# Keys in memory as three parts, maxima ahead of the operand loads, and a prologue that loads step 0 first

## The reference

```python
# x: 16 x 256 x 128, ctx: 16 x 1601 x 128; 16 heads of depth 8; all f32
qh, kh, vh = heads(layernorm(x) @ wq.T + bq), heads(ctx @ wk.T + bk), heads(ctx @ wv.T + bv)
attn = softmax(qh @ kh.T / sqrt(8))                 # per batch and head: 256 x 1601
x = x + tanh(g_xattn) * ((attn @ vh) @ wd.T + bd)
n = layernorm(x)
scores = sigmoid(n @ gate_W) * route_scale          # 8 experts, the best 2 of them
gate = one_hot_weights(top_k(scores, 2))            # divided by their sum
x = x + tanh(g_ffn) * (sum_e gate_e * (gelu(n @ W1_e + b1_e) @ W2_e + b2_e) + gelu(n @ Ws1 + bs1) @ Ws2 + bs2)
```

## Time and profile before

| | |
|---|---|
| median of three runs | 1434.74 us |
| profiled execution, own time | 1436.73 us |
| its span | 1434.9 us |
| PE busy | 1241.7 us (87%) |
| DVE busy | 1049.3 us (73%) |
| ACT busy | 1055.6 us (74%) |
| POOL busy | 418.7 us (29%) |
| mean granted clock of TensorE | 0.902 |
| moved by DMA | 147.13 MB, queue q1 47.4% of 16 engines |
| k_op<-k_dram | 64 transfers of 600.4 KB, 9.5 us from issue to landing |
| q_dram<-q_parts | 96 of 64.0 KB, 2.1 us |

### The profile page before, as it was taken

How to read it: one execution, slowest core, us unless ns; L and a number is a source line. 1 busy time by engine, 2 the same in 40 slices (tenths; PEclk the granted TensorE clock), 3 DMA queues, 4 the chain that set the end, 5 groups by cost and what they waited for, 6 DMA issues and landing times.

```text
span 1434.9 us, 29778 instructions
## 1 busy us (share of the span) xinstructions
PE 1241.7 (87%) x11555; PEld 458.9 (32%) x11555; DVE 1049.3 (73%) x1208; ACT 1055.6 (74%) x1962; POOL 418.7 (29%) x309
## 2 busy tenths in 40 slices
PE   2448889798989999899989999799979999799855
PEld 1112323232323433243323333243323433243224
DVE  8477778587768888688868878688768868689001
ACT  1008879587978799688968789688968889689741
POOL 7242224051333215151424125051423205010111
PEclk6568999798988999899989999899989999899786
DMA  7673634636273653737273744637173744501101
GB/s 213 114 149 69 150 70 98 140 84 129 53 164 70 139 119 87 147 81 149 52 169 61 170 87 99 139 82 146 47 167 67 165 92 96 102 11 33 31 14 45
DMA packets 71390, 147.13 MB, mean 103 GB/s; under 512 B 13705, under 2 KB 37970, under 8 KB 71250
## 3 DMA queue, kind: packets, MB, share of 16 engines
q1 hardware_dynamic: 71250, 145.24, 47.4%
HBM read 88.30 MB, written 56.91 MB: 101 GB/s over the span
## 4 chain that ended last, share of the span: by engine, by line
PE 66%; DMA 14%; ACT 5%; DVE 4%; SPq 4%; POOL 3%; issue 2%; POOLq 0%; ACTq 0%; DVEq 0%
PE o_ps L775 26%; PE a_ps L757 15%; PE b_ps L741 11%; DMA m_dram<-nm_parts 10%; PE a_ps L688 4%; PE a_ps L692 4%; ACT probs L573 3%; PE b_ps L720 2%; DVE run_max L901 2%; SPq L406 2%; DMA q_op<-m_dram 1%; SPq L397 1%; PE a_ps L684 1%; PE b_ps L723 1%; DMA q_op<-q_dram 1%
## 5 line engine op out<-in xcount | busy, mean ns | idle before, releaser
L901 DVE TENSOR_REDUCE run_max<-b_ps 128x2 f32<-128x1024 f32 x768 | 899.4, 1218 | 249.4 <-PE b_ps L741 246.0
L573 ACT ACTIVATE probs<-a_ps 128x512 f32<-128x512 f32 (+1 forms) x1664 | 901.9, 594 | 144.3 <-PE a_ps L757 127.4
L775 PE MATMUL o_ps<-probs,v_op 128*32 128x256 f32 (+3 forms) x4928 | 505.8, 483 | 2.3 <-ACT probs L573 1.2
L757 PE MATMUL a_ps<-q_op,k_op 51*128 51x256 bf16 (+1 forms) x3328 | 338.1, 283 | 46.4 <-DMA q_op<-m_dram 25.6
L741 PE MATMUL b_ps<-k_op,q_op 48*128 48x512 bf16 (+1 forms) x2048 | 325.6, 350 | 37.5 <-DVE run_max L901 24.2
L757 PEld LDWEIGHTS a_ps<-q_op,k_op 51*128 51x128 bf16 (+1 forms) x3328 | 112.9, 97 | 373.5 <-ACT probs L573 307.3
L741 PEld LDWEIGHTS b_ps<-k_op,q_op 48*128 48x128 bf16 x2048 | 88.7, 96 | 208.2 <-DVE run_max L901 95.9
L775 PEld LDWEIGHTS o_ps<-probs,v_op 128*32 128x32 f32 (+1 forms) x4928 | 98.4, 109 | 176.4 <-issue 93.8
L509 POOL TENSOR_TENSOR attn<-num,den_all 128x256 f32<-128x256 f32 x16 | 11.6, 728 | 440.3 <-DMA den_all<-r_dram 440.3
L688 PE MATMUL a_ps<-kctx,wk_s 128*128 128x400 f32 (+1 forms) x128 | 81.4, 734 | 55.7 <-DMA kctx<-ctx_t 49.9
L469 POOL TENSOR_TENSOR nm_parts<-nm_t,one 8x256 bf16<-8x256 f32 x32 | 19.3, 602 | 360.5 <-ACT nm_t L605 360.5
(11 more groups left out here) (100 smaller groups left out, 680.4 us busy)
## 6 DMA issues: line engine op xcount, KB each, us to landing
k_op<-k_dram SPq DMA_DIRECT2D x64, 600.4 KB, 9.5
k_dram<-k_parts SPq DMA_DIRECT2D x32, 600.4 KB, 6.0
kctx<-ctx_t SPq DMA_DIRECT2D x16, 800.5 KB, 12.5
...
```

The source lines that it names most:

```text
L573: act.activation(probs[0:keys, unit % PB, :], a_ps[at % AB][0:keys, :], ACT.Exp, scale=SCALE).then_inc(a_taken, 1)
L757: last = pe.matmul(a_ps[(at + side) % AB][0:KEYS[t], SEQ * a:SEQ * a + SEQ], k_op[buf][rows, slot, 128 * t:128 * t + KEYS[t]], q_op[buf][r ...
L775: last = pe.matmul(o_ps[32 * j:32 * j + 32, cols], v_op[s // 2 % 2][0:KEYS[t], t, GP * (s % 2) + j, :], probs[0:KEYS[t], unit % PB, cols], ...
L901: dve.tensor_reduce(run_max[:, t, :, p, c:c + 1].rearrange("q v o -> q (v o)"), slot[:, :, :], AX.X, ALU.max).then_inc(b_taken, 1)
```

## The change

It has four parts.

- k_dram holds each of the three parts of the keys once. store_keys makes two transfers of 64 x 3 x 1601 in place of six. load_operands reads the places of a side in three transfers, of 24, 16 and 8 rows, each of which starts at part 0. An operand load is eight transfers in place of four.
- On SyncE move_maxima(s+1) stands ahead of load_operands(s+3) in odd steps; in even steps the order of these two is as before. The load of the K context moves from the odd step to the even one, behind the maxima.
- The prologue loads only the first chunk of tokens at first; then come the keys' stores, the operands of step 0, the next K context, one chunk of tokens, the operands of step 1, the V context and the other tokens. The first query stores are issued by ScalarE.
- The order of units in steps -2 and -1 is changed on all engines: five S units come first in step -2, and in step -1 all S units of step 0 come first, then T.

```diff
--- before
+++ after
 FULL = GP * QTILES * RUNS
 SUNITS = FULL + QTILES
 S_AHEAD = 10
-OP_DMAS = 4
+OP_DMAS = 2 * (len(PLACES) + 1)
 OUT_DMAS = 3
-PART_STORES = 2 * len(PLACES)
+PART_STORES = 2
...
 
+def first_maxima():
+
+    scores = [event for event in ORDER[-2] if event[0] == "S"]
+    rest = [event for event in ORDER[-2] if event[0] != "S"]
+    first = [event for event in ORDER[-1] if event[0] == "S" and event[1] < SUNITS]
+    turn = [("A", ("T", 0, 0))]
+    return scores[:5] + rest + scores[5:], first + turn + [e for e in ORDER[-1] if e not in first + turn]
+
+
+ORDER[-2], ORDER[-1] = first_maxima()
...
         q_dram = nc.dram_tensor("q_dram", [BATCH, 2, len(QPART), 64, SEQ], BF16, kind="Internal").ap()
-        k_dram = nc.dram_tensor("k_dram", [2, 2, len(KPART), 64, CTX], BF16, kind="Internal").ap()
+        k_dram = nc.dram_tensor("k_dram", [2, 2, 3, 64, CTX], BF16, kind="Internal").ap()
...
 
-        key_in, first_in, const_in, x0_in, x_in, ones_set = (sem(n) for n in ("key_in", "first_in", "const_in", "x0_in",
-                                                                              "x_in", "ones_set"))
+        key_in, first_in, const_in, ones_set = (sem(n) for n in ("key_in", "first_in", "const_in", "ones_set"))
+        x_in = [sem(f"x_in{i}") for i in range(3)]
...
 
+        def store_queries(engine, c):
+
+            engine.wait_ge(q_chain, 4 * (c + 1))
+            for a in range(2):
+                for part, (r0, r1) in enumerate(PLACES):
+                    for r in range(r0, r1):
+                        engine.dma_start(q_dram[2 * c:2 * c + 2, a, r].rearrange("b r q -> r b q"),
+                                         q_parts[64 * a:64 * a + 64, part, :]
+                                         .rearrange("p (b q) -> p b q", b=2)).then_inc(q_written, 16)
+
...
@@ -307,13 +329,16 @@
             load(kctx, ctx_t[0]).then_inc(kctx_in, 16)
             for dst, src in keys:
                 load(dst, src).then_inc(key_in, 16)
-            sp.dma_start(x_s[:, 0:4, :], x[:, 0:4, :]).then_inc(x0_in, 16)
+            def load_tokens(c0, c1, arrived):
+
+                for c in range(c0, c1):
+                    sp.dma_start(x_s[:, 4 * c:4 * c + 4, :], x[:, 4 * c:4 * c + 4, :]).then_inc(arrived, 16)
+
+            load_tokens(0, 1, x_in[0])
             for dst, src in firsts:
                 load(dst, src).then_inc(first_in, 16)
             for dst, src in consts:
                 load(dst, src).then_inc(const_in, 16)
-            for c in range(1, CHUNKS):
-                sp.dma_start(x_s[:, 4 * c:4 * c + 4, :], x[:, 4 * c:4 * c + 4, :]).then_inc(x_in, 16)
...
@@ -329,8 +354,10 @@
                 for side in range(2):
                     rows = slice(SIDE * side, SIDE * side + ROWS)
                     pairs = slice(GP * g + 2 * side, GP * g + 2 * side + 2)
-                    sp.dma_start(k_op[buf][rows, :, :].rearrange("r (a p) c -> r a p c", a=2),
-                                 kd[:, :, pairs, :]).then_inc(op_in[buf], 16)
+                    for r0, r1 in PLACES:
+                        to = slice(SIDE * side + DH * r0, SIDE * side + DH * r1)
+                        sp.dma_start(k_op[buf][to, :, :].rearrange("r (a p) c -> r a p c", a=2),
+                                     kd[0:DH * (r1 - r0), :, pairs, :]).then_inc(op_in[buf], 16)
                     sp.dma_start(q_op[buf][rows, :, :].rearrange("r (a p) q -> r a p q", a=2),
                                  qd[:, :, pairs, :]).then_inc(op_in[buf], 16)
...
@@ -393,19 +420,8 @@
                     if s >= 0:
                         sp.wait_ge(op_in[s % 4], 16 * OP_DMAS * (s // 4 + 1))
                 for a in range(2):
-                    for r0, r1 in PLACES:
-                        sp.dma_start(k_dram[b % 2, a, r0:r1].rearrange("n r c -> r n c"),
-                                     k_parts[64 * a:64 * a + 64, 0:r1 - r0, :]).then_inc(k_written, 16)
...
-                                         .rearrange("p (b q) -> p b q", b=2)).then_inc(q_written, 16)
+                    sp.dma_start(k_dram[b % 2, a].rearrange("n r c -> r n c"),
+                                 k_parts[64 * a:64 * a + 64, :, :]).then_inc(k_written, 16)
...
                                  m_dram[h, :, GP * side:GP * side + GP, :]).then_inc(m_in[h], 16)
 
+            store_keys(0)
+            load_operands(0)
+            load_context("K", kctx, 1, kctx_in)
+            load_tokens(1, 2, x_in[1])
+            load_operands(1)
             load(vctx, ctx_t[0]).then_inc(vctx_in, 16)
-            store_keys(0)
-            load_context("K", kctx, 1, kctx_in)
-            store_queries(0)
-            load_operands(0)
+            load_tokens(2, CHUNKS, x_in[2])
             for s in range(FIRST, LAST + 1):
                 b = s // 2
                 if 0 <= s - 1 < STEPS:
                     move_outputs(s - 1)
                 if s % 2 == 1 and b + 2 < BATCH:
                     store_keys(b + 2)
-                if 0 <= s + 3 < STEPS:
+                if s % 2 == 0 and 2 <= s + 3 < STEPS:
                     load_operands(s + 3)
                 if s % 2 == 0 and 0 <= b - 1 < BATCH:
                     spread_sums(b - 1)
                 if s % 4 == 2 and 0 <= (s - 6) // 4 < CHUNKS:
                     spread_gates((s - 6) // 4)
-                if s % 2 == 1 and b + 3 < BATCH:
+                if 0 <= s + 1 < STEPS:
+                    move_maxima(s + 1)
+                if s % 2 == 1 and 2 <= s + 3 < STEPS:
+                    load_operands(s + 3)
+                if s % 2 == 0 and b + 3 < BATCH:
                     load_context("K", kctx, b + 3, kctx_in)
                 if s % 2 == 1 and 0 <= b + 2 < BATCH:
                     load_context("V", vctx, b + 2, vctx_in)
-                if 0 <= s + 1 < STEPS:
-                    move_maxima(s + 1)
                 if s % 4 == 3 and 0 < (s + 5) // 4 < CHUNKS:
-                    store_queries((s + 5) // 4)
+                    store_queries(sp, (s + 5) // 4)
...
                     act.activation(tgf[:, :], gf_s[:, :], ACT.Tanh).then_inc(tanh_done, 1)
                 aux_unit(*unit)
+            store_queries(act, 0)
             act.wait_ge(const_in, 16 * len(consts))
             act.wait_ge(ones_set, 2)
...
                 dve.wait_ge(bias_seq, 4)
-                dve.wait_ge(x_in, 16 * (CHUNKS - 1))
...
             dve.memset(k_op[0][:, :, :], 1.0).then_inc(k_ones[0], 1)
-            dve.wait_ge(x0_in, 16)
+            dve.wait_ge(x_in[0], 16)
...
                             add_ffn(unit[1], unit[2])
                         n += 1
                         if s % 4 == 2 and n == 2 and 0 < (s + 6) // 4 < CHUNKS:
+                            if s < 4:
+                                dve.wait_ge(x_in[s // 4 + 2], 16 if s < 0 else 16 * (CHUNKS - 2))
                             statistics("q", (s + 6) // 4)
```

7 lines of the change are left out of this document (removed).

## The result

The changed kernel takes 1492.0 us at the median (1488.6 to 1493.8, four runs) and the kernel before, run beside it, 1432.95. The ratio is 1.041, with a 95% interval of 1.036 to 1.046. So it is slower by about 59 us. The forecast was 1462, with a range up to 1485.

What follows compares the result with a forecast made beforehand. TensorE, busy 87% of the span, was taken to set the pace. Hand-overs +5.6 and +25.6 (together +31.2), prologue -3.5, gave +27.7 us on 1434.74: 1462 us; own range 1440 to 1485, 8-in-10 range 1398 to 1485.

Steps and rivals of the forecast that it cites:

- The maxima land 1.4 us after T in odd steps, the K context is there: At odd-to-even hand-overs: from SyncE's issue of the maxima store (T), landing takes 1.4 us and TensorE finds the K context.
- One operand load and one context, 14.3 us behind 2.0: SyncE's queue: after 2.0 us for the maxima and q_op loads, the o_dram store waits 14.3 us behind this bulk.
- B: The 7 hand-overs into steps 2, 6, ..., 26, maxima store to den reciprocal: forecast 191.3 us against 165.7, +25.6.
- The +3.0 us of the pieces: Each operand load, cut into 24, 16 and 8 partitions, was taken to last 3.0 us longer.
- VectorE's waits, 4 to 7 us: VectorE's reciprocal of den (R) would wait 4 to 7 us for num in each of the 14 hand-overs.
- A: The 7 hand-overs into steps 4, 8, ..., 28, maxima store to den reciprocal: forecast 206.3 us against 200.7, +5.6.
- Query stores in A, 3.0 us: Twelve query stores ahead of o_dram in SyncE's queue add 3.0 us; the last such hand-over has none.
- The clock, 3.0 us a place, 42 in all: Each VectorE wait is followed by 3.0 us lost to TensorE's lower granted clock, at the 14 hand-overs.
- Fewer stores gain nothing: Key stores at the start of odd steps, two a batch instead of six, were claimed to give no gain on the path.
- The prologue, -3.5: Before the steady steps: first probability scores at 107 instead of 110.81, a gain of 3.5 us.
- Rival 1: Operand load pieces overlap wholly, so a load still takes its 9.7 us: sum -31, 1404 us; chance 0.25.
- Rival 3: The old waits for kctx and the maxima go and nothing replaces them: 1337 us; chance 0.05.

Runs made afterwards that it cites:

- a1_order: Kernel before with only SyncE's loop order changed: in odd steps maxima ahead of the operand load, K context in even steps; 1396 us, ratio 0.973.
- e0_order_parts: Kernel before with SyncE's new order and the three-part keys in pieces of 24, 16 and 8, prologue of before; 1467 us, ratio 1.023.
- b1_pieces: a1_order with each operand side loaded in pieces of 24, 16 and 8 partitions, keys in six places, six stores; 1480 us, ratio 1.031.
- h1_early: Kernel before with three-part keys in 16-partition pieces, odd-step load right behind the key stores, contexts and queries in even steps behind the spread sums; 1348 us, ratio 0.939.
- a3_prologue: Kernel before with only the changed prologue (ScalarE query stores, tokens in three loads, step 0's needs first, new score order); 1435 us, ratio 1.001.
- p1_value_first: Changed kernel with one prologue line moved: batch 0's V context loaded ahead of the operands of step 1; 1475 us, ratio 1.028.
- a2_parts: Kernel before with only three-part keys, two stores, and operand sides loaded in pieces of 24, 16 and 8 partitions; 1414 us, ratio 0.986.
- a4_noparts: Changed kernel without the three parts: keys in six places, operand sides loaded whole, order and prologue changed; 1401 us, ratio 0.978.

## Why the prediction was wrong, step by step

The direction was right, and so was the path: the waits for kctx and the maxima go, the output chain stands behind the load and the V context, and VectorE waits in all 14 hand-overs. The amount was half of what was measured, and the time fell outside the range. Two sizes failed, both by the same term, the pieces; a third, the clock, made up for part of it.

- **The maxima land 1.4 us after T in odd steps, the K context is there:** right in all 14.
- **One operand load and one context, 14.3 us behind 2.0:** a little short. Without pieces (a1_order) the outputs of B are in memory at T+18.0, where the working gives 2.0 + 14.3 + 0.6 = 16.9, or 17.5 with the out store. No row shows the 2.4 us of latency that the working takes out of the 14.3 (a small store with nothing ahead landed in 1.4), but the sum uses it in the prologue alone.
- **The +3.0 us of the pieces: this is the step that failed.** Alone a load got 3.6 us longer (12.0 to 15.6), close to the forecast; but with the V context behind it the outputs landed 4.7 us later in both kinds (a1_order to e0_order_parts; with the load alone cut, in b1_pieces, 4.3 to 4.4). In the changed kernel the outputs landed at T+23.1 at the mean of the 14, where the sum had 21.4. These 1.7 us are about 24 of the 30 us by which T to R came out above the forecast's 355.6 (185.3 + 170.3); most of the other 6 is a landing to reciprocal of 4.4 us instead of 4.0. The reason given for the term, that the rate goes with the partitions in flight, was not tested as such.
- **VectorE's waits, 4 to 7 us:** 7.3 to 12.5 us in A and 4.8 to 8.5 in B. Besides the late landing, VectorE stood earlier in A than the working had it: with no wait R comes at T+16.7 in h1_early, not at T+19.5 (B: 19.6, forecast 19.8).
- **Query stores in A, 3.0 us:** about right as a term, from one case. The six A hand-overs with them have o_dram at T+23.8 at the mean, the one without at T+20.9 (forecast 22.9 and 19.9). They didn't wait in the queue only: their issue took SyncE 9.1 to 14.2 us instead of 7.7 to 8.5, and o_dram was itself issued late.
- **The clock, 3.0 us a place, 42 in all:** too much, and as a cost not shown. R to the next T grew by 28.6, but TensorE also stood 23.7 us longer in these stretches (38.1 against 14.4), 1.5 us each time from the reciprocal to its next matmul (1056.27 and 1057.76). The clock did fall behind R. But counted as time x (1 - granted clock) over the 14 hand-overs, the loss only changed places: behind R it was 1.7 us before and 49.9 after, between T and R 70.0 before and 26.9 after. And h1_early, with 11.9 lost behind R and no wait for num, took 789.1 us from R to the next T, as long as the changed kernel (787.4). What the lower clock costs here stays open.
- **"Fewer stores gain nothing":** doubtful. In the new order they came out 12 us faster (b1_pieces to e0_order_parts, intervals that overlap), and in the old one they let the load start 6 us earlier against T.
- **The prologue, -3.5:** wrong by 15 us, mostly by the same term. From the issue of the load for step 0 to the V context's arrival 32.1 us were forecast and 41.4 measured. With whole loads (a3_prologue, issue at 40.00) it took 26.9, where the same sum without pieces gives 26.1. So the two loads in pieces cost 14.5 us there, some 7 each instead of 3.0. The first score came 17.9 us behind its load instead of 14.9 (11.8 with whole loads). The load for step 0 left at 34.72 instead of 31.8, as ScalarE's issue took 12.03 us for the twelve, the upper bound of the working. The V context's place behind the load for step 1 had also not been questioned; p1_value_first shows that this place cost 17 us.
- **What I didn't see at all:** that the parts gain in the old order, 18 us in a2_parts. The sum did put the pieces on the path in 14 places of the new order, but it gave the two stores nothing, and it never asked what the parts do where the load's length is covered.

The V unit of a3_prologue, with whole loads:

```profile
66.87 2.05 PE L710 MATMUL a_ps<-wv_s,vctx 128*128 128x128 f32 x8 [5.85 <-DMA vctx<-ctx_t]
```

Rival 1 is close to a kernel without pieces: it said 1404, and a4_noparts took 1401. Part of that is luck. Its T to R without the clock is 313.6 us and measured 319.0, but its prologue was 13 us too early (-9.5, measured +3.5), and its clock loss of 31.5 us stands against 9.4 more from R to the next T. So of the 30 us between forecast and result nearly all lies in the pieces (58 us forecast from rival 1 to the forecast, 91 measured from a4_noparts to the changed kernel). Rival 3's 1337 wasn't reached by this order; h1_early, with another, came within 11 us of it.
